# One slot of an embedding gather shared between GpSimd and SyncE

## The reference

```
emb_cat  = cat_t2[f, cat_feats]                     # 2048 x 26 rows of 64 floats
first    = sum(cat_t1[f, cat_feats]) + sum(cont_t1 * cont_feats)
E        = concat([emb_cat, cont_t2 * cont_feats])  # 2048 x 39 x 64
fm       = 0.5 * sum(sum(E)**2 - sum(E*E))
h        = relu(batchnorm(E.reshape(2048, 2496) @ W1 + b1))   # to 1024
h        = relu(batchnorm(h @ W2 + b2))                       # to 512
out      = sigmoid(bias + first + fm + h @ W3 + b3)
```

## Time and profile before

| | |
|---|---|
| median of 3 runs | 871.62 us (866.34 to 873.04) |
| span of the profiled execution | 645.4 us |
| difference of the two | 226.2 us |
| TensorE, VectorE, ScalarE, GpSimd busy | 522.1, 216.2, 191.7, 399.0 us |
| gathers of GpSimd | 416, the first at 5.80 us, the last at 529.39 us |

### The profile page before, as it was taken

How to read it: one execution, slowest core, us unless ns; L and a number is a source line. 1 busy time by engine, 2 the same in 40 slices (tenths; PEclk the granted TensorE clock), 3 DMA queues, 4 the chain that set the end, 5 groups by cost and what they waited for, 6 DMA issues and landing times.

```text
span 645.4 us, 9108 instructions
## 1 busy us (share of the span) xinstructions
PE 522.1 (81%) x3324; PEld 467.0 (72%) x3324; DVE 216.2 (33%) x428; ACT 191.7 (30%) x405; POOL 399.0 (62%) x423
## 2 busy tenths in 40 slices
PE   0839999969766977698679966997698778999993
PEld 0139989968766877687577956796688777788882
DVE  1362252214221422142205220522052235654366
ACT  1351231212111211121113110321031225897655
POOL 5787777777777777777777777777777760000000
PEclk9958997997999798979987999788979878999996
DMA  8963234323332333234323432333234520000000
GB/s 284 296 133 28 29 28 28 27 26 27 27 28 25 28 27 26 27 28 27 27 27 26 27 28 27 26 28 26 27 27 60 123 25 0 2 1 1 1 0 1
DMA packets 18021, 26.74 MB, mean 41 GB/s; under 512 B 7602, under 2 KB 7834, under 8 KB 18010
## 3 DMA queue, kind: packets, MB, share of 16 engines
q0 software_dynamic: 13312, 13.87, 27.5%
q1 hardware_dynamic: 4384, 12.66, 5.5%
q10 hardware_dynamic: 314, 0.07, 0.1%
HBM read 26.56 MB, written 0.02 MB: 41 GB/s over the span
## 4 chain that ended last, share of the span: by engine, by line
POOL 54%; issue 19%; PE 16%; DMA 4%; DVE 3%; ACT 3%; POOLq 0%; SPq 0%; DVEq 0%; ACTq 0%
POOL emb L249 54%; PE bank L696 10%; DMA h<-in_w 4%; PE bank L631 2%; PE bank L658 2%; ACT h L388 1%; PE bank L681 1%; DMA emb<-in_table,idx_now 1%; DVE h L612 0%; DVE stats L557 0%; ACT hhi L351 0%; PE bank L731 0%; DVE stats L490 0%; DVE mv L544 0%; DVE zpart L592 0%
## 5 line engine op out<-in xcount | busy, mean ns | idle before, releaser
L249 POOL DMA_INDIRECT emb<-in_table,idx_now x416 | 398.2, 957 | 130.7 <-issue 130.7
L658 PE MATMUL bank<-xhi,w1hi 128*128 128x256 f32 x832 | 254.6, 306 | 0.0
L658 PE MATMUL bank<-xlo,w1hi 128*128 128x256 f32 x832 | 245.4, 295 | 0.0
L658 PE MATMUL bank<-xhi,w1lo 128*128 128x256 f32 x832 | 244.9, 294 | 0.0
L658 PEld LDWEIGHTS bank<-xhi,w1hi 128*128 128x128 f32 x832 | 170.0, 204 | 0.0
L658 PEld LDWEIGHTS bank<-xlo,w1hi 128*128 128x128 f32 x832 | 170.0, 204 | 0.0
L658 PEld LDWEIGHTS bank<-xhi,w1lo 128*128 128x128 f32 x832 | 169.1, 203 | 0.0
L442 DVE TENSOR_TENSOR xlo<-bank,xhi 128x256 fp32r<-128x256 f32 x104 | 44.0, 423 | 351.6 <-ACT xhi L282 351.6
L282 ACT ACTIVATE xhi<-bank 128x256 fp32r<-128x256 f32 x104 | 39.8, 383 | 377.4 <-PE bank L646 377.4
L646 PE MATMUL bank<-ident,emb 128*128 128x128 f32 x208 | 45.6, 303 | 76.7 <-DMA emb<-in_table,idx_now 74.8
L646 PEld LDWEIGHTS bank<-ident,emb 128*128 128x128 f32 x208 | 23.7, 146 | 93.0 <-DMA emb<-in_table,idx_now 85.3
(11 more groups left out here) (68 smaller groups left out, 288.1 us busy)
## 6 DMA issues: line engine op xcount, KB each, us to landing
h<-in_w SPq DMA_DIRECT2D x13, 512.0 KB, 16.0
emb<-in_table,idx_now POOLq DMA_INDIRECT x416, 3.3
h<-in_w SPq DMA_DIRECT2D x1, 3072.0 KB, 12.6
w2raw<-in_w SPq DMA_DIRECT2D x8, 256.0 KB, 5.5
h<-in_w SPq DMA_DIRECT2D x1, 256.0 KB, 13.4
idx_all<-in_cat SPq DMA_DIRECT2D x1, 208.0 KB, 2.8
cont_sb<-in_cont_t SPq DMA_DIRECT2D x8, 13.0 KB
diag<-in_cont_diag ACTq DMA_DIRECT2D x1, 45.5 KB, 3.0
```

The lines of the kernel that those rows point to most:

```text
L249: nc.gpsimd.indirect_dma_start(out=emb[:, j, at:at + ROW], out_offset=None, in_=table, in_offset=bass.IndirectOffsetOnAxis(ap=idx_now[:, j ...
L658: done = nc.tensor.matmul(acc[c], w[:, k, cols], x[:, s, :], start=False, stop=(last and n == 2), skip_group_check=True)
```

## The change

The last of a block's 52 slots (pair 12, tile 1, half 1) is split. GpSimd's indirect DMA writes partitions 0 to 63 alone. The 64 rows of partitions 64 to 127 are fetched by SyncE: it reads 16 indices at a time from SBUF into registers, and issues one transfer of one row for each. Their indices come in through a new input of 2 KB on one partition (`rows_idx`), which VectorE clamps and offsets at the start in four instructions (`find_own_rows`). SyncE begins when these are done and waits for `summed` and `squared` of the last group in every block, as GpSimd does. In the last block it issues 32 rows, then the eight transfers of `W2`, then the other 32. TensorE waits for the rows of SyncE too before it transposes pair 12.

```diff
+ROWS_K, ROWS_J, ROWS_HALF = KT - 1, BT - 1, 1
+ROWS_AT = 64
+NROWS = P - ROWS_AT
+ROWS_READ = 16
+ROWS_BEFORE_W2 = 32
...
+    rows_idx = nc.alloc_sbuf_tensor_at("rows_idx", [P, BLOCKS * NROWS], i32, offset=m_at)
...
         def _(sp):
             sp.dma_start(idx_all[:, :], cat).then_inc(idx_in, 16)
+            sp.dma_start(rows_idx[ROWS_AT:ROWS_AT + 1, :], cat_rows).then_inc(rows_idx_in, 16)
...
-            with sp.Fori(0, BLOCKS) as b:
+            def cont_load(b):
                 sp.wait_ge(cont_used, b + EMPTY)
                 sp.dma_start(cont_sb[:, :], cont_t[:, ds(b * BC, BC)]).then_inc(cont_in, 16)
+            def rows_open(b):
+                g = len(GROUPS) - 1
+                sp.wait_ge(summed[g], b + EMPTY)
+                sp.wait_ge(squared[g], BT * b + EMPTY)
+            def gather_rows(b, first, end):
+                at = ROWS_K * PAIR + ROWS_HALF * ROW
+                for r0 in range(first, end, ROWS_READ):
+                    _, rows = nc.values_load_multi_w_load_instructions(
+                        rows_idx[ROWS_AT:ROWS_AT + 1, ds(b * NROWS + r0, ROWS_READ)],
+                        engines=(mybir.EngineType.SP,), min_val=0, max_val=CAT * VOCAB - 1,
...
+                    for i, row in enumerate(rows):
+                        p = ROWS_AT + r0 + i
+                        sp.dma_start(emb[p:p + 1, ROWS_J, at:at + ROW],
+                                     table[ds(row, 1), :]).then_inc(rows_gathered, 16)
+            sp.wait_ge(rows_step, ROWS_STEPS)
+            with sp.Fori(0, BLOCKS - 1) as b:
+                cont_load(b)
+                rows_open(b)
+                gather_rows(b, 0, NROWS)
+            b = BLOCKS - 1
+            cont_load(b)
+            rows_open(b)
+            gather_rows(b, 0, ROWS_BEFORE_W2)
             s = W2RAW_KT % XT
             sp.wait_ge(x_used[s], X_USES[s] * (BLOCKS - 1) + W2RAW_KT // XT + 1 + EMPTY)
             for k in range(C1):
                 sp.dma_start(w2raw[:, k, :], w2[k * P:(k + 1) * P, :]).then_inc(w2_in, 16)
+            gather_rows(b, ROWS_BEFORE_W2, NROWS)
...
+                                n = ROWS_AT if (k, j, half) == (ROWS_K, ROWS_J, ROWS_HALF) else P
                                 nc.gpsimd.indirect_dma_start(
-                                    out=emb[:, j, at:at + ROW], out_offset=None, in_=table,
-                                    in_offset=bass.IndirectOffsetOnAxis(ap=idx_now[:, j, f:f + 1], axis=0),
+                                    out=emb[0:n, j, at:at + ROW], out_offset=None, in_=table,
+                                    in_offset=bass.IndirectOffsetOnAxis(ap=idx_now[0:n, j, f:f + 1], axis=0),
...
+            def find_own_rows():
+                x, w = rows_idx[ROWS_AT:ROWS_AT + 1, :], rows_w[ROWS_AT:ROWS_AT + 1, :]
+                dve.wait_ge(rows_idx_in, 16)
+                nc.vector.tensor_scalar(w, x, 0, VOCAB, ALU.is_lt, ALU.mult).then_inc(rows_step, 1)
...
                     pe.wait_ge(gathered[k], 16 * 2 * BT * (b + 1))
+                    if k == ROWS_K:
+                        pe.wait_ge(rows_gathered, 16 * NROWS * (b + 1))
```

More of the change, by code:

```diff
@@ L44, with build @@
 FM_STEPS = 8
+ROWS_K, ROWS_J, ROWS_HALF = KT - 1, BT - 1, 1
+ROWS_F = 2 * ROWS_K + ROWS_HALF
+ROWS_AT = 64
+NROWS = P - ROWS_AT
+ROWS_READ = 16
+ROWS_BEFORE_W2 = 32
 PAR = 3 * C1 + 4 * C2 + 2
-def build(nc, table, cat, cont_t, cont_tab, cont_diag, w1, w2, params, out):
+def build(nc, table, cat, cat_rows, cont_t, cont_tab, cont_diag, w1, w2, params, out):
     f32, f32r = mybir.dt.float32, mybir.dt.float32r
@@ L75, in build @@
     xlo = place("xlo", [P, XT, BC], f32r)
+    m_at = cursor[0]
     m_sb = place("m_sb", [CONT, H1], f32)
@@ L103, in build @@
     bn1 = place("bn1", [P, 5, C1], f32)
+    rows_idx = nc.alloc_sbuf_tensor_at("rows_idx", [P, BLOCKS * NROWS], i32, offset=m_at)
+    rows_w = nc.alloc_sbuf_tensor_at("rows_w", [P, BLOCKS * NROWS], i32, offset=m_at + 4 * BLOCKS * NROWS)
     kt_bytes = H1 * 4
@@ L157, in build @@
         group_open = sem("group_open")
+        rows_idx_in, rows_step, rows_gathered = sem("rows_idx_in"), sem("rows_step"), sem("rows_gathered")
         m_done, m_ready = sem("m_done"), sem("m_ready")
@@ L184, in build @@
         out_done = sem("out_done")
+        ROWS_STEPS = 4
         TP_USES = [len(range(s, KT, TP)) for s in range(TP)]
@@ L212, in _ @@
                 sp.dma_start(raw[:, raw_slot(k), :], w1[k * P:(k + 1) * P, :]).then_inc(raw_in[k], 16)
-            with sp.Fori(0, BLOCKS) as b:
+            def cont_load(b):
                 sp.wait_ge(cont_used, b + EMPTY)
                 sp.dma_start(cont_sb[:, :], cont_t[:, ds(b * BC, BC)]).then_inc(cont_in, 16)
+            def rows_open(b):
[8 more added lines that the diff above has]
+                        engines=(mybir.EngineType.SP,), min_val=0, max_val=CAT * VOCAB - 1,
+                        skip_runtime_bounds_check_because="the vector engine clamps them")
+                    for i, row in enumerate(rows):
[11 more added lines that the diff above has]
+            gather_rows(b, 0, ROWS_BEFORE_W2)
             s = W2RAW_KT % XT
@@ L433, in _ @@
                 stage_indices(g, 0)
+            def find_own_rows():
+                x, w = rows_idx[ROWS_AT:ROWS_AT + 1, :], rows_w[ROWS_AT:ROWS_AT + 1, :]
+                dve.wait_ge(rows_idx_in, 16)
+                nc.vector.tensor_scalar(w, x, 0, VOCAB, ALU.is_lt, ALU.mult).then_inc(rows_step, 1)
+                dve.wait_ge(rows_step, 1)
+                nc.vector.tensor_tensor(w, w, x, ALU.add).then_inc(rows_step, 1)
+                dve.wait_ge(rows_step, 2)
+                nc.vector.tensor_scalar(w, w, 0, VOCAB - 1, ALU.max, ALU.min).then_inc(rows_step, 1)
+                dve.wait_ge(rows_step, 3)
+                nc.vector.tensor_scalar(x, w, ROWS_F * VOCAB, None, ALU.add).then_inc(rows_step, 1)
+            find_own_rows()
             for k in range(KT):
@@ L749 @@
     cat = np.ascontiguousarray(x["r_cat_feats"].reshape(P, TILES * CAT))
+    own = x["r_cat_feats"].reshape(P, BLOCKS, BT, CAT)[ROWS_AT:, :, ROWS_J, ROWS_F]
     cont_t = np.ascontiguousarray(x["r_cont_feats"].reshape(P, TILES, CONT).transpose(2, 1, 0).reshape(CONT, BATCH))
@@ L757 @@
     arrays = {
-        "table": table.reshape(CAT * VOCAB, ROW), "cat": cat, "cont_t": cont_t, "cont_tab": cont_tab,
+        "table": table.reshape(CAT * VOCAB, ROW), "cat": cat, "cat_rows": own.T.reshape(1, BLOCKS * NROWS),
+        "cont_t": cont_t, "cont_tab": cont_tab,
         "cont_diag": cont_diag.reshape(P, CONT_KT * CONT), "w1": x["W1"], "w2": x["W2"],
```

## The result

The changed kernel takes 910.34 us (median of 4 runs, 908.34 to 913.06), the kernel before 870.33 in the same comparison (4 runs, 866.34 to 873.04). The ratio is 1.045 (95% interval 1.042 to 1.049): the change costs 40 us, 4.5%, and the forecast of 869.5 us (864 to 884) was wrong. A ratio in this document goes by the runs within 1.5% of the fastest of their kernel; that leaves out two runs in all, both of the half-rows version of experiment 2.

The account below looks back on a forecast made before the run. The prediction took GpSimd's gather pace as the bound, with SyncE's rows hidden: -2.4 us from shorter gathers plus 0.3 for VectorE makes the span 643.3, and with 226.2 us around it 869.5 us (range 864 to 884).

Parts of the forecast that it names:

- The bound: GpSimd's unbroken string of gathers, 1.25 us each, 64.9 us a block, sets the time; SyncE's 39 us a block is hidden.
- With the 226.2 us around it unchanged: Time outside the profiled span, added unchanged to the forecast span of 643.3 us to give 869.5 us.
- The 64-row gather: GpSimd's 52nd gather of each block, halved to 64 rows, saves 0.3 us; eight make -2.4 us (0 to -5.0).
- Rival 2: On GpSimd, a gather of 64 rows costs as much as one of 128: 871.9 us; chance 0.16.
- The sum's gain of 2.1 us: On the span, -2.4 us from GpSimd's gathers plus 0.3 from VectorE: 645.4 to 643.3 us.
- A row on SyncE: Transfer with address arithmetic 0.44 us plus index read 0.17 us; 64 rows make 39 us a block, ends 30 and 118.
- Its landing: SyncE's last row of a block lands 2.8 us after issue, taken from the idx_all load.
- Rival 1: SyncE becomes the bound at pair 12's wait for its rows; 942 us at 1.01 us a row; chance 0.15.
- its limit of 0.87: SyncE's rows are in time for pair 12 of the last block if each takes under 0.87 us, 55.8 us a block.
- VectorE's four instructions: At the start, about 2 us in VectorE's idle time; charged +0.3 us once (0 to 0.5) for holding GpSimd up.
- Rival 4: The program around the span grows with SyncE's longer code and the added input; 1% either way; chance 0.06.
- The late load of `cont_sb`: Queued on SyncE behind the 64 rows, 39 us into the block, some 20 us before TensorE needs it: costs nothing.

Follow-up runs that it names:

- experiment 2: Changed kernel with SyncE fetching 32 rows of the slot instead of 64 and GpSimd gathering 96; ratio 1.028 against the kernel before.
- experiments 9: The changed kernel without any edit, on a chip where the kernel before takes 649.09 us: 649.19 us, ratio 1.0002.
- experiment 11: Changed kernel with GpSimd's 52nd gather dropped, SyncE fetching 96 rows and ScalarE 32: 953.48 against 869.96 us on one chip, 640.04 against 648.90 on another.
- experiment 10: Changed kernel with a different piece of SyncE work per block (single transfer, increments, fixed rows, real rows): 648.22 us on one chip, 915.18 against 869.96 on another.
- the version with rows set aside: Changed kernel with SyncE's rows sent to unused memory, GpSimd gathering all 128 rows and TensorE not waiting for SyncE: 1025.69 us, ratio 1.179.
- experiments 5 to 7: Changed kernel with fixed-address transfers, with instructions but no transfers, or with one 64-row transfer: 648.47, 648.29 and 647.31 us where the kernel before took 648.70.

## Why the prediction was wrong

**The bound: this is the step that failed.** The prediction read "no wait for a free group ever holds GpSimd up" and "TensorE is busy 51.0 of 64.9", and concluded that whatever SyncE does "counts only if pair 12 of a block comes in later". All of that holds for the profile that it was read from, and experiments 9 and 11 confirm it on that kind of chip. On the chips that gave the times TensorE sets the block, slowed beside the gathers, and there SyncE's work isn't hidden: it takes starts from TensorE, 71 matmuls beside 16 gathers instead of 91 (experiment 10 shows the same inside one execution). It should have cost 0 and costs 40 us, 5.0 a block.

**"With the 226.2 us around it unchanged"** carried the error in. A quarter of the time was unexplained, and I put it outside the program without a row for it. The program's start and end can't hold it: in every execution whose time and span are both known the two differ by 1.7 to 1.8 us. The front's own numbers couldn't say this; they did say that the profile and the time might not be of the same thing, and none of my rivals was that.

**The 64-row gather** was mis-sized. I guessed 0.3 us won, and it is 0.04 (0.94 to 0.90), 8 x 0.04 = 0.3 us in all instead of 2.4. Rival 2 was right in substance. The sum's gain of 2.1 us isn't there even on the 649 kind, to which its rows belong: the ratio is 1.0002 (0.998 to 1.0023), and the last gather starts at 530.29, against 527.3 forecast and 529.39 before. The Trainium skill, "DMA: Bandwidth & Descriptors", section "Anatomy of one DMA — SWDGE (gpsimd) path", says that many descriptors can be emitted before the incremental cost shows; the 0.04 us for 64 rows agrees.

**A row on SyncE** was 0.44 + 0.17 = 0.61 us, and on the 649 kind it is 0.41 (37, 29 and 228 ns and what lies between) plus 1.137 / 16 = 0.07 for its index: 31.5 us a block, against 39. On the 870 kind it is 1.03, taken over a block's rows. Its landing, which I took as 2.8 us from the load of `idx_all`, is 1.0 (experiment 11). The Trainium skill, "DMA: Bandwidth & Descriptors", section "Latency and other measured facts", gives a tensor_load a floor of about 600 ns; the load of 1.137 us agrees with it. The estimate that I made from it, a floor for every row, doesn't hold, as one load brings 16 indices.

**Rival 1** had the right sign and half of its premise: on the 870 kind a row does cost 1.03 us, above its limit of 0.87. But that limit came from a block of 64.9 us, a block there is 99, and pair 12 wasn't kept waiting; in the version of experiment 11, with 96 rows, it was. **VectorE's four instructions** took 2 us as said. **Rival 4**, growth around the span, is gone with the 226 us. **The late load of `cont_sb`** (506.12, behind the rows) is in time, as the prediction had it; behind the 109 us of the version with rows set aside it was not. DMA engines are busy 23% in the block.

**Open.** What makes TensorE and SyncE start instructions some 0.7 us apart or more beside gathers on one kind of chip and not on the other, and whether the kind belongs to the chip; how the 5 us a block divides between SyncE's instructions and its transfers; how it goes with the number of rows. The three variants of experiments 5 to 7 never ran whole on a chip of the 870 kind.

## What to carry to other kernels

Before a forecast, set the span of the profile against the time of its own execution; if they differ by more than the few us of starting up, profile and times may be of different conditions, and then no engine's slack in the profile counts for the times. "Hidden beside a bound" needs the bound of the execution that is timed: work on an idle queue cost nothing here under one bound and 5 us a block under the other. Read the chain of an experiment's own profile before its time: the version with rows set aside looked like more of the same loss, and had another bound. A 128-row gather is paid for almost entirely as an instruction (0.94 us, against 0.90 for 64 rows), so take away whole gathers or none. To compare stretches of two executions, take the same piece of work in both (here a string of 16 or 20 gathers), not windows picked by eye.

## What the hardware showed that I hadn't expected

- One program takes 649 us on some chips and 870 on others, each steady within 1% in its one set of runs. On the slower ones TensorE's instructions start some 0.7 or 1.4 us apart beside GpSimd's gathers, with no releaser, and SyncE's MOVE (29 ns at the median) reaches 1.40 us.
- On a slower one, 192 semaphore increments of SyncE that nobody waits for go with 35 matmuls of TensorE beside 20 gathers, where it is 66 with a single transfer (one profiled execution, two blocks of each).
- Transfers of a row with a register in the destination's offset: 26 packets for 260 bytes, 784 ns at the median, against 2 packets and 228 ns with a fixed destination.
- A load of 16 registers from SBUF took 1.13 to 1.23 us in all 32 cases of the changed kernel on the 649 kind.
